# Moving one flag's sum and branch, two query splits, halves of exactness looks, loads and two blocks' attention in a fused attention and feed-forward kernel

## The chip, the cores and the metric

One core of a Trainium2 chip. Its engines run side by side and meet only through semaphores: TensorE (PE; PEld is its weight load), VectorE (DVE), ScalarE (ACT), GpSimd (POOL) and SyncE (SP, which issues the DMAs). The time is device microseconds of one launch; a smaller one is better. Of the kernel before there are three runs, 651.85 to 653.5 us, median 653.43.

## The reference

One post-norm layer on x of 4096 x 256. The attention is linear: K'V is summed over all tokens before any output can be formed. The feed-forward part is gated, with two hidden layers of 1024 x 1024 whose weights are -1, 0 or 1 times a factor.

```python
Q, K, V = x@wq.T, x@wk.T, x@wv.T
context = (Q @ einsum('bnd,bne->bde', K, V)) * sqrt(3/64)
x = layernorm(x + context @ wo.T)
h = silu(tlin(x, w1, s1)) * tlin(x, w2, s2)     # 256 -> 1024
h = gelu(tlin(h, h1, sh1))                      # 1024 -> 1024
h = gelu(tlin(h, h2, sh2))
x = layernorm(x + tlin(h, w3, s3))              # 1024 -> 256
```

## The kernel before

**Tiles.** The 4096 tokens are 8 blocks of 512 (four row tiles of 128), worked on in four pairs p = 0 to 3. Matmuls run in a rounded fp32 format. To keep fp32 accuracy, each operand that is not a weight is a high part (rounded by ScalarE, `hi`, L674, or `hi_of_q`, L618, `hi_of_transposed`, L625) and a low part (the rest, by VectorE, `lo`, L944, `lo_of_q`, L874, `lo_of_transposed`, L885), and each weight tile meets both.

**The hidden layers** (l = 0, 1 of a pair) take seven half-size products in place of eight, as Strassen's scheme does: a weight matrix of 1024 x 1024 is cut in 2 x 2 parts, GpSimd makes sums of those parts once (`combine(i)`, units 0 to 7: four for each hidden weight) and differences of activations in each pair (`differences`, L506 and L516, `further_differences`, L525 and L528). SyncE stores the sums in `combos` in HBM (`store_unit`), copies the plain halves there by `relay_hidden`, and loads one product's weights, 1 MB, into one of three ring slots (`load_ring(g)`). A product is 4 column tiles of 8 matmuls of 512 columns (L1322). Products 0 to 6 of hidden layer L alternate between bank groups B and A; ScalarE copies some out (`copy_out`, L690), VectorE adds others (L951, L957, L963), ScalarE applies gelu (L720).

**Flags.** [...] ScalarE looks: an activation with an accumulated sum of low halves (L569), `bits_of_whole(i)` on a loaded unit (1.06 us), `bits_of_sums(i)` on GpSimd's sums in a long and a short part. For each of seven flags TensorE sums the looks (`flag_sum(s)`, L1211), VectorE turns the sum into a bit (`flag_out(s)`, L866 and L868), and TensorE loads the bit (L1217), compares and branches (L1230): the stage that follows is in the program in an exact and in a plain form. With the reference's data all flags take the exact form. In source order the stages are `front`, `first_l1` and the halves of the first pair's hidden layers.

**The front.** Loads, keys and values, the query projection in 32 pieces, block 0's attention, its residual, layer norm tile by tile (`normalised_tilewise`, VectorE; two of the four last steps are ScalarE's, L631), its transposes (`transposed_first(q)`, L1194) and block 1's attention in two halves. Then `first_l1` runs the gated first layer for blocks 0 and 1: 16 tiles of 4 matmuls (L1262) each, to four banks, with silu (L640) and gate (L938) behind them; a tile's bank must be free, so tile t waits for silu or gate (t - 4)/2. Blocks 2 and 3 get attention and residual (`residual1`, L891) inside pair 0, as later blocks do in the pair before theirs.

**What sets the order.** Every engine's program is written out by hand in one order, with waits on semaphores; nothing is scheduled later. SyncE's queue is in order as well, so a DMA behind a waiting one is late. The change edits these orders.

Of the kernel before, what the change touches and what calls it, by code (L numbers as in the profile page):

```python
# [81 lines left out]
def build(nc, xT_in, xr_in, wkv_src, wq_in, wo_in, w1_in, w2_in, h1_in, h2_in, w3_src, sc_in, s3_in, out):  # L82
# [4 lines left out]
    with ctx:  # L87
# [93 lines left out]
        hidden_relayed = [sem(f"hidden_relayed{l}") for l in range(2)]  # L181
# [92 lines left out]
        def _(sp):  # L274
# [32 lines left out]
            def relay_hidden(l):  # L307

                src = sources[l].rearrange("p (h i n) -> p h i n", h=2, i=KH)[:, :, :, 0:HALF]
                for h in range(2):  # L310
                    sp.dma_start(combos[:, l, 5 + h, :, :], src[:, h, :, :]).then_inc(hidden_relayed[l], 16)
# [12 lines left out]
            def load_ring(g):  # L324
# [3 lines left out]
                if L < 2 and n == 0:  # L328
                    sp.wait_ge(hidden_relayed[L], 32)
# [47 lines left out]
            relay_hidden(1)  # L377
            load_ring(4)
            load_rows_late(2)
            load_ring(5)  # L380
# [178 lines left out]
        def _(act):  # L559
# [162 lines left out]
            def hidden(p, l):  # L722
# [5 lines left out]
                if L == 0:  # L728
                    bits_of_whole(5)
# [83 lines left out]
            for j in range(HC):  # L813
                silu(0, j, A)
                if j == 1:
                    hi_of_q(2)
                if j == 3:
                    hi_of_q(3)
                if j == 0:
                    bits_of_whole(2)  # L820
                if j == 2:
                    bits_of_sums(0)
# [4 lines left out]
                if j == 6:  # L827
                    bits_of_whole(3)
            for j in range(HC):
                silu(1, j, A)  # L830
                if j == 0:
                    bits_of_sums(1)
                if j < KH:
                    hi(0, 1, j)
                if j == 1:
                    bits_of_whole(4)
                if j == 4:
                    bits_of_sums(2)
# [24 lines left out]
        def _(dve):  # L863
# [101 lines left out]
            def hidden(p, l):  # L965
# [91 lines left out]
            def normalised_tilewise(ln, b, add):  # L1057
                y = xr[:, b % 4, :].rearrange("p (t e) -> p t e", e=E)

                for q in range(TPB):  # L1060
# [4 lines left out]
                    nc.vector.bn_aggr(mv[ln][:, ln, q, :], st[ln][:, ln, q, :]).then_inc(tile_aggr[ln], 1)  # L1065
                for q in range(ACT_TILES[ln], TPB):
# [15 lines left out]
            normalised_tilewise(0, 0, attention_residual)  # L1082
            flag_out(1)
# [3 lines left out]
            for j in range(HC):  # L1087
# [3 lines left out]
                if j == 1:  # L1091
                    lo_of_q(2)
                if j == 2:
                    normalise(0, 1, 1)
                if j == 3:
                    lo_of_q(3)
# [36 lines left out]
        def _(pe):  # L1133
# [164 lines left out]
            def product(p, l, n, view):  # L1298
# [3 lines left out]
                for j in range(KH):  # L1302
# [22 lines left out]
                    last.then_inc(prod, 1)  # L1325

# [8 lines left out]
            def with_sums(p, l, view):  # L1335
# [81 lines left out]
            def front(view):  # L1417
# [18 lines left out]
                q_pieces(range(23, 28), view)  # L1436
                pe.wait_ge(q_raw, 2)
# [4 lines left out]
                pe.wait_ge(tile_sum[0], 1)  # L1442
                flag_sum(1)
                transposed_first(2)
                attention_half(0)
                transposed_first(3).then_inc(tr_ready, 1)
                attention_half(1).then_inc(op_ready, 1)
# [12 lines left out]
            def first_l1(view):  # L1460
# [9 lines left out]

                l1(0, A, view, side)
# [60 lines left out]
```

## Time and profile before

| | |
|---|---|
| runs, median (lowest to highest) | 653.43 us (651.85 to 653.5) |
| the profiled execution, its span | 653.65 us, 651.9 us |
| mean granted TensorE clock | 0.998 of full speed |
| TensorE busy | 637.2 us, 98% |
| VectorE, ScalarE, GpSimd busy | 485.7, 410.7, 282.1 us |
| DMA share, 60 to 110 us | 0.92 to 1.03 |

The span runs from the first instruction to the last. A timeline row gives start and duration in us, engine, line, operation, what it writes and reads, the shapes, how many instructions are merged, and in brackets the engine's idle time before it and what ended it. Matmuls overlap: one of 512 columns is shown with 0.39 us and the next starts 0.23 us after it. "issue" is idle time that ended by nothing the profile shows.

### The profile page before, as it was taken

Reading aid. Unit: us, or ns where it says so; the run is one execution under the profiler, and the core shown is the slowest. Engines: PE = TensorE matmul, PEld = TensorE weight load, DVE = VectorE, ACT = ScalarE, POOL = GpSimd, SP = SyncE. Lnnn points to the kernel's source line nnn. Section 1 sums busy time; section 2 is a strip of 40 time slices with the busy share of each in tenths; the row PEclk is TensorE's granted clock in tenths of the full one; section 3 lists DMA queues with packets and bytes.
Section 4 is the critical chain, followed back from the end, with each engine's and each line's share of the span. In section 5 each row is a group of like instructions: output and inputs, shape, how many; then the busy total and the mean of one; then the engine's idle time right before and its main releaser. Section 6 shows DMA issues by size and latency. Waiting matters only on the chain.

```text
span 651.9 us, 9251 instructions
## 1 busy us (share of the span) xinstructions
PE 637.2 (98%) x3191; PEld 534.6 (82%) x3191; DVE 485.7 (75%) x717; ACT 410.7 (63%) x696; POOL 282.1 (43%) x226
## 2 busy tenths in 40 slices
PE   8989999999999999999999999999999999999995
PEld 6867788878889888888889888888889888888885
DVE  4677598789664997798655898698754899488476
ACT  5488789658761666557662657656763457666554
POOL 0367999295000663097000565079000367068034
PEclk9999999999999999999999999999999999999999
DMA  8989999764320036633330035734330015444201
GB/s 327 394 325 341 372 380 348 285 255 164 130 67 1 1 118 220 211 130 130 130 129 1 1 97 167 250 126 168 130 129 2 1 28 188 173 135 160 94 1 66
DMA packets 24370, 103.89 MB, mean 159 GB/s; under 512 B 2224, under 2 KB 3312, under 8 KB 16496
## 3 DMA queue, kind: packets, MB, share of 16 engines
q1 hardware_dynamic: 24032, 102.98, 44.5%
q8 instruction: 29, 0.48, 0.3%
q10 hardware_dynamic: 288, 0.26, 0.1%
q14 instruction: 21, 0.17, 0.1%
HBM read 87.51 MB, written 23.07 MB: 170 GB/s over the span
## 4 chain that ended last, share of the span: by engine, by line
PE 72%; DVE 3%; POOL 1%; issue 1%; ACT 1%; POOLq 0%; DVEq 0%; ACTq 0%
PE ps L1322 49%; PE ps L1262 13%; PE ps L1376 8%; DVE R L944 1%; DVE xr L928 1%; PE ps L1194 1%; PE ps L1182 1%; PE ps L1399 0%; ACT R L674 0%; DVE U L963 0%; POOL rstd L488 0%; POOL quarter L516 0%; ACT quarter L720 0%; POOL rstd L459 0%; POOL quarter L525 0%
## 5 line engine op out<-in xcount | busy, mean ns | idle before, releaser
L1322 PE MATMUL ps<-R,ring 128*128 128x512 f32 x1792 | 410.1, 390 | 1.6 <-DVE fsum L866 1.2
L1322 PEld LDWEIGHTS ps<-R,ring 128*128 128x128 f32 x1792 | 335.2, 188 | 71.6 <-DVE fsum L866 1.6
L944 DVE TENSOR_TENSOR R<-quarter,R 128x512 fp32r<-128x512 f32 x284 | 261.8, 944 | 62.6 <-ACT R L674 62.2
L674 ACT CAST R<-quarter 128x512 fp32r<-128x512 f32 x288 | 175.4, 616 | 30.6 <-POOL quarter L516 12.6
L1262 PE MATMUL ps<-x1T,w 128*128 128x512 f32 x512 | 119.4, 391 | 1.9 <-ACT sg L640 1.1
L720 ACT ACTIVATE quarter<-U,sc 128x512 f32<-128x512 f32 x96 | 69.5, 724 | 74.2 <-DVE U L963 29.4
L1262 PEld LDWEIGHTS ps<-x1T,w 128*128 128x128 f32 x512 | 95.2, 188 | 23.8 <-ACT sg L640 2.7
L506 POOL TENSOR_TENSOR quarter<-quarter,quarter 128x512 f32<-128x512 f32 x32 | 49.6, 1550 | 97.8 <-ACT quarter L720 91.1
L457 POOL TENSOR_TENSOR ve<-mv,eps 128x4 f32<-128x4 f32 x14 | 5.7, 404 | 181.5 <-DVE mv L921 181.5
L640 ACT ACTIVATE sg<-ps,sc 128x512 f32<-128x512 f32 x64 | 44.0, 689 | 61.3 <-PE ps L1262 61.1
L690 ACT COPY U<-ps 128x512 f32<-128x512 f32 x96 | 56.3, 586 | 31.3 <-PE ps L1322 31.3
L938 DVE SCALAR_TENSOR_TENSOR quarter<-ps,sc,sg 128x512 f32<-128x512 f32 x64 | 47.8, 746 | 23.7 <-ACT sg L640 13.4
L516 POOL TENSOR_TENSOR quarter<-quarter,quarter 128x512 f32<-128x512 f32 x32 | 48.9, 1527 | 16.7 <-DVE quarter L938 12.9
L1376 PEld LDWEIGHTS ps<-w,R 128*128 128x128 f32 x448 | 54.7, 192 | 0.7 <-DVE R L944 0.2
L1376 PE MATMUL ps<-w,R 128*128 128x256 f32 x448 | 55.1, 283 | 0.0
L528 POOL TENSOR_TENSOR quarter<-quarter,quarter 128x512 f32<-128x512 f32 x32 | 50.0, 1594 | 0.0
L525 POOL TENSOR_TENSOR quarter<-quarter,quarter 128x512 f32<-128x512 f32 x32 | 48.8, 1554 | 0.0
L928 DVE TENSOR_SCALAR xr<-xr,mv,rstd 128x256 f32<-128x256 f32 x52 | 35.5, 743 | 4.2 <-POOL rstd L459 4.2
L957 DVE TENSOR_TENSOR U<-ps,U 128x512 f32<-128x512 f32 x32 | 22.0, 690 | 14.7 <-PE ps L1322 14.7
L720 ACT ACTIVATE quarter<-ps,sc 128x512 f32<-128x512 f32 x32 | 22.1, 691 | 12.6 <-PE ps L1322 12.6
L963 DVE TENSOR_TENSOR U<-ps,U 128x512 f32<-128x512 f32 x32 | 21.8, 685 | 8.2 <-PE ps L1322 8.2
L446 POOL TENSOR_TENSOR beside<-unit 128x512 f32<-128x512 f32 x8 | 12.2, 1530 | 29.8 <-ACT junk L569 27.7
(84 smaller groups left out, 383.4 us busy)
## 6 DMA issues: line engine op xcount, KB each, us to landing
ring<-combos SPq DMA_DIRECT2D x56, 1024.0 KB, 4.9
combos<-unit SPq DMA_DIRECT2D x8, 1024.0 KB, 7.1
unit<-in_h1T SPq DMA_DIRECT2D x4, 1024.0 KB, 13.9
xr<-in_x_rows SPq DMA_DIRECT2D x8, 512.0 KB, 6.2
unit<-in_h2T SPq DMA_DIRECT2D x4, 1024.0 KB, 12.7
xT<-in_xT SPq DMA_DIRECT2D x7, 512.0 KB, 8.6
out<-xr SPq DMA_DIRECT2D x7, 512.0 KB, 2.9
w<-w_dram SPq DMA_DIRECT2D x3, 1024.0 KB, 7.5
```

What stands on the lines that cost most here:

```text
L506: nc.gpsimd.tensor_tensor(x12[:, c, :], x12[:, c, :], x11[:, c, :], ALU.subtract).then_inc(t_done, 1)
L516: nc.gpsimd.tensor_tensor(t2[:, c, :], x22[:, c, :], x12[:, c, :], ALU.subtract).then_inc(t_done, 1)
L525: nc.gpsimd.tensor_tensor(x11[:, c, :], t2[:, c, :], x11[:, c, :], ALU.subtract).then_inc(t_done, 1)
L528: nc.gpsimd.tensor_tensor(x21[:, c, :], x21[:, c, :], t2[:, c, :], ALU.subtract).then_inc(t_done, 1)
L674: nc.scalar.copy(R[slot_of(p, u)][:, 0, c, :], quarter[operand_home(p, u)][:, c, :]).then_inc(hi_done, 1)
L690: nc.scalar.copy(U[:, 1 if i == 2 else 0, j, :], ps[:, B + j, :]).then_inc(cp_done, 1)
L720: nc.scalar.activation(quarter[dst][:, j, :], src, ACT.Gelu, scale=sc[:, 2 + l, chunk:chunk + 1]).then_inc(gelu_done, 1)
L938: nc.vector.scalar_tensor_tensor(quarter[dst][:, j % KH, :], ps[:, base + (2 * j + 1) % 4, :], sc[:, 1, j:j + 1], sg[:, j % 2, :], ALU.mul ...
L944: nc.vector.tensor_tensor(r[:, 1, c, :], quarter[operand_home(p, u)][:, c, :], r[:, 0, c, :].bitcast(f32), ALU.subtract).then_inc(lo_done, 1)
L1262: last = nc.tensor.matmul(ps[:, base + t % 4, :], w, view(x1T[beta % 2][:, part, c, :]), start=n == 0, stop=n == 2 * EC - 1)
L1322: last = nc.tensor.matmul(ps[:, bank + j, :], w, view(R[slot_of(p, u)][:, part, k, :]), start=n in (0, 1, 5) and k == 0 and part == 0, sto ...
L1376: last = nc.tensor.matmul(rows_of(b)[:, q, :], view(slot[:, part, k, q * P:(q + 1) * P]), w, start=first and k == 0 and part == 0 and q % ...
```

## The change

It moves work; apart from a finer semaphore (one per half of a relay) nothing is added or taken away.

- TensorE: `flag_sum(1)` before the first transpose of block 0; the last two transposes of block 0 and block 1's attention from the end of `front` to the start of `first_l1`, so behind flag 1's load and branch. In every pair but the last, attention of the next pair's blocks goes from behind product 5 to behind its third and its fourth tile.
- VectorE: `flag_out(1)` between the tile statistics and the last two normalisations; `lo_of_q(2)` and `(3)` from the first layer to the first adds of hidden layer 0; the first of its two residuals one step later.
- ScalarE: `hi_of_q(2)` and `(3)` to the same place; the two parts of each look at sums apart; looks at units 3 and 4 one step earlier and later.
- SyncE: relay halves apart, unit 3's store earlier, loads of units 5 and 7 and of the ring changed about.

```diff
-            relay_hidden(0)
+            relay_hidden(0, 0)
             load_unit(4)
             store_unit(2)
             load_ring(0)
+            relay_hidden(0, 1)
+            store_unit(3)
             load_ring(1)
+            load_ring(2)
             load_unit(5)
-            store_unit(3)
             load_unit(6)
-            load_ring(2)
+            load_ring(3)
             load_unit(7)
             store_unit(4)
-            load_ring(3)
-            relay_hidden(1)
             load_ring(4)
+            relay_hidden(1, 0)
             load_rows_late(2)
+            relay_hidden(1, 1)
...
@@ scalar, hidden(p, l)
                 if L == 0:
+                    hi_of_q(2)
+                    hi_of_q(3)
                     bits_of_whole(5)
...
@@ scalar, first layer
             for j in range(HC):
                 silu(1, j, A)
-                if j == 0:
-                    bits_of_sums(1)
+                if j <= 1:
+                    bits_of_sums(1, range(j, j + 1))
                 if j < KH:
                     hi(0, 1, j)
-                if j == 1:
+                if j == 2:
                     bits_of_whole(4)
-                if j == 4:
-                    bits_of_sums(2)
+                if 3 <= j <= 4:
+                    bits_of_sums(2, range(j - 3, j - 2))
...
@@ vector
+                    if L == 0 and j < 2:
+                        lo_of_q(a + j)
...
-                    if L == 0 and j == 1:
+                    if L == 0 and j == 2:
                         residual1(a, B)
...
-            normalised_tilewise(0, 0, attention_residual)
-            flag_out(1)
+            normalised_tilewise(0, 0, attention_residual, lambda: flag_out(1))
...
@@ tensor, with_sums
-                product(p, l, 5, view)
-                if l == 0 and more:
-                    for i in range(2):
-                        pe.wait_ge(gelu_done, n_gelu(L, 1, 2 * i + 1))
-                        attention_out(a + i, lambda q, at=B + 2 * i: ps[:, at + q // 2, q % 2 * E:(q % 2 + 1) * E])
+
+                def attention(j):
+                    if j >= 2:
+                        pe.wait_ge(gelu_done, n_gelu(L, 1, 2 * j - 3))
+                        attention_out(a + j - 2, lambda q, at=B + 2 * (j - 2): ps[:, at + q // 2, q % 2 * E:(q % 2 + 1) * E])
+
+                product(p, l, 5, view, attention if l == 0 and more else None)
...
```

TensorE at the end of the front, before. L1145 are pieces of the query projection, L1211 is flag 1's sum, L1194 a tile's transpose, L1182 half of block 1's attention, and the last three rows are the flag's load and branch:

```order
L1194 MATMUL ps<-ident,xr 128x128 x2
L1145 MATMUL ps<-xhi_112,wqr 128x512 x2
L1194 MATMUL ps<-ident,xr 128x128 x2
L1145 MATMUL ps<-xlo_120,wqr 128x512 x2
L1211 MATMUL ps<-lowf,ones 1x4
L1194 MATMUL ps<-ident,xr 128x128 x2
L1182 MATMUL ps<-T1s,qs_66 128x256 x4
L1194 MATMUL ps<-ident,xr 128x128 x2
L1182 MATMUL ps<-T1s,qs_66 128x256 x4
L1217 TENSOR_LOAD flag
L1217 ISA x2
L1230 COMPARE_AND_BRANCH
```

The same place after; the lines have moved by two:

```order
L1209 MATMUL ps<-lowf,ones 1x4
L1192 MATMUL ps<-ident,xr 128x128 x2
L1143 MATMUL ps<-xhi_112,wqr 128x512 x2
L1192 MATMUL ps<-ident,xr 128x128 x2
L1143 MATMUL ps<-xlo_120,wqr 128x512 x2
L1215 TENSOR_LOAD flag
L1215 ISA x2
L1228 COMPARE_AND_BRANCH
L1192 MATMUL ps<-ident,xr 128x128 x2
L1180 MATMUL ps<-T1s,qs_66 128x256 x4
L1192 MATMUL ps<-ident,xr 128x128 x2
L1180 MATMUL ps<-T1s,qs_66 128x256 x4
```

The sum has moved up by four rows, and load and branch stand ahead of the third transpose.

ScalarE in block 1's first layer, before, from its first silu (L640) on. L569 are looks: unit_125 is unit 4 as loaded, unit_122 and beside_130 are the long and the short part of unit 1's sums; L674 is a high part:

```order
L640 ACTIVATE sg<-ps,sc 128x512
L569 ACTIVATE junk,lowf<-unit_122 128x2048
L569 ACTIVATE junk,lowf<-beside_130 128x512
L674 CAST R_60<-quarter_53 128x512
L640 ACTIVATE sg<-ps,sc 128x512
L674 CAST R_60<-quarter_53 128x512
L569 ACTIVATE junk,lowf<-unit_125 128x1024
L640 ACTIVATE sg<-ps,sc 128x512
L674 CAST R_60<-quarter_53 128x512
L640 ACTIVATE sg<-ps,sc 128x512
L674 CAST R_60<-quarter_53 128x512
L640 ACTIVATE sg<-ps,sc 128x512
```

The same place after:

```order
L570 ACTIVATE junk,lowf<-unit_122 128x2048
L675 CAST R_60<-quarter_53 128x512
L641 ACTIVATE sg<-ps,sc 128x512
L570 ACTIVATE junk,lowf<-beside_130 128x512
L675 CAST R_60<-quarter_53 128x512
L641 ACTIVATE sg<-ps,sc 128x512
L675 CAST R_60<-quarter_53 128x512
L570 ACTIVATE junk,lowf<-unit_125 128x1024
L641 ACTIVATE sg<-ps,sc 128x512
L675 CAST R_60<-quarter_53 128x512
L570 ACTIVATE junk,lowf<-unit_123 128x2048
L641 ACTIVATE sg<-ps,sc 128x512
```

The look at unit 4 has changed sides with the third silu, and the long look at unit 2's sums (unit_123), which followed the fifth silu, now stands ahead of it.

## Rows read from the trace of the kernel before

**Rows 1.** The page, part 1: busy us, share of the span, instructions.

```profile
PE 637.2 (98%) x3191; PEld 534.6 (82%) x3191; DVE 485.7 (75%) x717; ACT 410.7 (63%) x696; POOL 282.1 (43%) x226
```

**Rows 2.** Waits of TensorE, whole span: us in total, times, longest.

```profile
PE ps L1194 <- ACT xr L631: 1.4, 1, 1.4
...
PE ps L1322 <- DVE fsum L866: 1.2, 1, 1.2
```

**Rows 3.** Timeline, 35 to 42 us: start, duration, instruction, idle before.

```profile
37.50 0.18 DVE L1065 BATCH_NORM_AGGREGATE mv<-st 128x2 f32<-128x6 f32 x1
...
38.79 0.44 PE L1194 MATMUL ps<-ident,xr 128*128 128x128 f32 x2
...
39.55 0.38 PE L1194 MATMUL ps<-ident,xr 128*128 128x128 f32 x2
...
39.96 1.07 ACT L625 CAST x1T<-ps 128x512 fp32r<-128x512 f32 x2 [0.67 <-PE ps L1194]
...
40.58 1.29 DVE L885 TENSOR_TENSOR x1T<-ps,x1T 128x512 fp32r<-128x512 f32 x2 [1.13 <-ACT x1T L625]
...
41.08 1.34 PE L1262 MATMUL ps<-x1T,w 128*128 128x512 f32 x4 [0.68 <-ACT x1T L625]
```

**Rows 4.** Line 1217, flag loads: ns min/median/max, starts; all, then 39:41.

```profile
L1217 PEldq TENSOR_LOAD <-flag x7: 298/493/1169, 8.7 to 181.9; - x7
...
L1217 PEldq TENSOR_LOAD <-flag x1: 906/906/906, 39.5 to 39.5; - x1
```

**Rows 5.** Timeline of ScalarE, 57 to 76 us.

```profile
57.88 0.69 ACT L640 ACTIVATE sg<-ps,sc 128x512 f32<-128x512 f32 x1 [0.29 <-PE ps L1262]
58.47 1.90 ACT L569 ACTIVATE junk<-unit 128x2048 uint8<-128x2048 uint16 x1
...
60.49 0.63 ACT L569 ACTIVATE junk<-beside 128x512 uint8<-128x512 uint16 x1
...
61.12 0.60 ACT L674 CAST R<-quarter 128x512 fp32r<-128x512 f32 x1
61.63 0.68 ACT L640 ACTIVATE sg<-ps,sc 128x512 f32<-128x512 f32 x1
...
63.77 1.06 ACT L569 ACTIVATE junk<-unit 128x1024 uint8<-128x1024 uint16 x1 [0.95 <-DMA unit<-in_h2T]
```

**Rows 6.** Timeline of TensorE, from 51 us on.

```profile
51.24 13.23 PE L1262 MATMUL ps<-x1T,w 128*128 128x512 f32 x56
65.55 4.85 PE L1262 MATMUL ps<-x1T,w 128*128 128x512 f32 x20 [1.08 <-ACT sg L640]
...
73.86 5.72 PE L1322 MATMUL ps<-R,ring 128*128 128x512 f32 x24 [0.39 <-issue]
...
79.63 38.38 PE L1322 MATMUL ps<-R,ring 128*128 128x512 f32 x168
```

**Rows 7.** Timeline of VectorE, 70 to 74 us: flag 2.

```profile
71.61 0.14 DVE L866 TENSOR_REDUCE fsum<-ps 1x1 f32<-1x4 f32 x1
71.79 0.14 DVE L868 TENSOR_SCALAR flag<-fsum 1x1 int32<-1x1 f32 x1
```

**Rows 8.** Line 944, low parts: ns min/median/max; then VectorE's timeline, 62 to 96 us.

```profile
L944 DVE TENSOR_TENSOR R<-quarter,R x284: 660/692/1831, 54.4 to 640.3; 128x512 fp32r<-128x512 f32 x142
...
91.71 4.91 DVE L944 TENSOR_TENSOR R<-quarter,R 128x512 fp32r<-128x512 f32 x3 [0.20 <-ACT R L674]
```

**Rows 9.** Line 333, ring loads' landing: issued 40 to 120 us, then at 97.8.

```profile
DMA to landing us min/median/max: 5.3/9.4/13.3
...
DMA to landing us min/median/max: 8.6/8.6/8.6
```

**Rows 10.** Timeline of VectorE, 112 to 142 us.

```profile
119.00 1.23 DVE L891 TENSOR_TENSOR xr<-ps,xr 128x1024 f32<-128x1024 f32 x1 [2.78 <-PE ps L1182]
...
125.55 0.15 DVE L866 TENSOR_REDUCE fsum<-ps 1x1 f32<-1x4 f32 x1 [0.59 <-PE ps L1211]
...
137.71 3.92 DVE L944 TENSOR_TENSOR R<-quarter,R 128x512 fp32r<-128x512 f32 x4
```

More of the change, by code:

```diff
@@ L180, in build @@
         unit_out = [sem(f"unit_out{i}") for i in range(NU)]
-        hidden_relayed = [sem(f"hidden_relayed{l}") for l in range(2)]
+        hidden_relayed = [[sem(f"hidden_relayed{l}_{h}") for h in range(2)] for l in range(2)]
         ring_in = [sem(f"ring_in{k}") for k in range(SLOTS)]
@@ L305, in load_w12, with relay_hidden @@
                 sp.dma_start(w12[:, at:at + EC * HID].bitcast(f32), w12_dram[:, at:at + EC * HID]).then_inc(w12_in[i], 16)
-            def relay_hidden(l):
+            def relay_hidden(l, h):
                 src = sources[l].rearrange("p (h i n) -> p h i n", h=2, i=KH)[:, :, :, 0:HALF]
-                for h in range(2):
-                    sp.dma_start(combos[:, l, 5 + h, :, :], src[:, h, :, :]).then_inc(hidden_relayed[l], 16)
+                sp.dma_start(combos[:, l, 5 + h, :, :], src[:, h, :, :]).then_inc(hidden_relayed[l][h], 16)
             def load_unit(i):
@@ L327, in load_ring @@
                     sp.wait_ge(prod, n_prod((g - SLOTS) // NPROD, (g - SLOTS) % NPROD, KH - 1))
-                if L < 2 and n == 0:
-                    sp.wait_ge(hidden_relayed[L], 32)
+                if L < 2 and n < 2:
+                    sp.wait_ge(hidden_relayed[L][n], 16)
                 if L < 2 and n == 2:
@@ L814, in _ @@
                 silu(0, j, A)
-                if j == 1:
-                    hi_of_q(2)
-                if j == 3:
-                    hi_of_q(3)
                 if j == 0:
                     bits_of_whole(2)
-                if j == 2:
-                    bits_of_sums(0)
+                if 2 <= j <= 3:
+                    bits_of_sums(0, range(j - 2, j - 1))
                 if j == TR1_AFTER:
@@ L826, in _ @@
                     hi(0, 0, j - KH)
-                if j == 6:
+                if j == 5:
                     bits_of_whole(3)
@@ L1055, in _, with normalised_tilewise @@
                                            ALU.mult, ALU.subtract).then_inc(t1_lo, 1)
-            def normalised_tilewise(ln, b, add):
+            def normalised_tilewise(ln, b, add, between=None):
                 y = xr[:, b % 4, :].rearrange("p (t e) -> p t e", e=E)
@@ L1065, in normalised_tilewise @@
                     nc.vector.bn_aggr(mv[ln][:, ln, q, :], st[ln][:, ln, q, :]).then_inc(tile_aggr[ln], 1)
+                if between is not None:
+                    between()
                 for q in range(ACT_TILES[ln], TPB):
@@ L1090, in _ @@
                     stats(0, 1, 1)
-                if j == 1:
-                    lo_of_q(2)
                 if j == 2:
                     normalise(0, 1, 1)
-                if j == 3:
-                    lo_of_q(3)
                 if j > KH:
@@ L1296, in bank_free, with product @@
                     pe.wait_ge(add_done, n_add(L, 1, j))
-            def product(p, l, n, view):
+            def product(p, l, n, view, side=None):
                 L, u = 2 * p + l, NPROD * l + n
@@ L1325, in product @@
                     last.then_inc(prod, 1)
+                    if side is not None:
+                        side(j)
             def hidden(p, l, view):
@@ L1436, in front @@
                 q_pieces(range(23, 28), view)
+                pe.wait_ge(tile_sum[0], 1)
+                flag_sum(1)
                 pe.wait_ge(q_raw, 2)
@@ L1441, in front @@
                 q_pieces(range(30, 32), view)
[L1442 to L1447, printed above, removed]
             def transposed_first(q):
@@ L1469, in flag_side @@
                         flag_sum(2)
+                transposed_first(2)
+                attention_half(0)
+                transposed_first(3).then_inc(tr_ready, 1)
+                attention_half(1).then_inc(op_ready, 1)
                 l1(0, A, view, side)
```

1 line of the change is left out of this document (removed).

## The prediction

> **What bounds the kernel now.** I read the page first. TensorE is busy 98% of the span [rows 1], so a change of order can only win back TensorE's idle time or make more of it. Then I read TensorE's waits: they are few, and all but the last few tenths of a microsecond lie in the first 142 us [rows 2, 3, 6]. Those inside the stretch that the change touches are
>
> - 1.4 us for the first normalised tile of block 0 [rows 2],
> - 0.68 us before the first layer of block 0 [rows 3],
> - 1.08 us inside the first layer of block 1, for a silu [rows 6],
> - 0.39 us ("issue") before the first hidden product [rows 6],
> - 1.2 us in the second product of the second hidden layer, for flag 5's sum on VectorE [rows 2].
>
> That is 4.7 us of 651.9, or 0.7%; no order can give more. The rest of the kernel runs at the matmul's own pitch: 168 matmuls in 38.38 us, 0.228 us each, 7.3 us a product [rows 6]. So each edit is judged by what it does to one of these five waits. The timelines show who is late at each.
>
> **Flag 1, front.** Before, TensorE's program for the front ends with the two last transposes and block 1's attention, and then reads flag 1 and branches. After, it reads the flag and branches first; the transposes come behind the branch. The third tile's transpose ran at 38.79, the fourth's at 39.55, ScalarE's copy at 39.96, the first layer at 41.08 [rows 3]. The order now has the flag between VectorE's last aggregate (ends 37.68 [rows 3]) and the last two normalisations. Reduce and compare take 0.32 us from 71.61 to 71.93 [rows 7], so the bit is there at about 38.0, when TensorE's sequencer has just issued its last projection pieces. The sum itself moves into the 1.4 us wait and costs nothing there; it saved 0.12 us only on a path that no longer decides.
>
> The flag's load costs: seven loads took 0.30 to 1.17 us, and the one in this place 0.91 us, from 39.5 to 40.4 [rows 4]. From the load's end at 40.40 to the first matmul at 41.08 [rows 3] are 0.68 us of compare, branch and first weights. So the third transpose can start at 38.0 + 0.91 + 0.68 = 39.6 instead of 38.79: 0.8 us late. All that follows on the same chain (fourth transpose, ScalarE's two copies, VectorE's low parts, first layer) is late by the same. The gap of 0.68 us before the first layer does not pay for this: the branch was waited for there, but VectorE's low half, needed for the layer's fourth matmul, was itself only ready at 41.87 [rows 3], so that without the branch 0.16 us at most was to be had. With the shortest and the longest load the lateness is 0.2 and 1.06 us. I take 0.8, the row of this very load.
>
> The Trainium skill (DMA: Bandwidth & Descriptors, Latency and other measured facts) gives a tensor load a floor of about 600 ns. By that the lateness is 38.0 + 0.6 + 0.68 - 38.79 = 0.5 us, an estimate from that page. The trace disagrees with a floor: its fastest load took 298 ns [rows 4].
>
> **ScalarE in block 1's first layer.** Before, the look at unit 4 stood ahead of the third silu and waited 0.95 us for the unit's DMA [rows 5]; TensorE then waited 1.08 us for that silu, and the row of 56 matmuls ahead of it had lost 0.3 us against its pitch [rows 6]. After, that look stands behind the third silu, and the two-part looks at the sums are cut in halves. I walk the new queue with the distances between starts in rows 5: silu to next 0.59, long half 2.02, short half 0.63, cast to next 0.51, look at a unit 1.06. silu 0 at 57.88, long half 58.47, cast 60.49, silu 1 61.00, short half 61.59, cast 62.22, silu 2 62.73, cast 63.32, look at unit 4 63.83 (its data were there at 63.75 even in the old DMA order, so no wait), silu 3 64.89, cast 65.48, long half 65.99, silu 4 68.01, which ends at 68.70. When does TensorE want them? Its matmul after the old wait started at 65.55; 1.08 idle, the 0.16 by which a modelled end lies behind the pitch, and the 0.3 lost before it go off: 64.0 for the third silu. That now ends at 63.4, so the wait goes. But the fifth is wanted 16 matmuls later, at 67.7, and there TensorE waits until 68.75: 1.05 us come back, because the long half now stands ahead of the fifth silu and not behind it. 16 matmuls and flag 2's sum (0.12) more, and the layer ends at 72.6 by the pitch, before at 73.3 (the first product's 73.86 less the 0.39 of idle time and the 0.16): 0.7 us gained. Ends: 1.4 us, if that second wait does not show, and 0, if it is as long as both old ones. I take 0.7, the walk.
>
> **Flag 2.** Its gate now follows the sixth silu at 69.23, and ends at 70.7; the bit is there at 71.0, before at 71.93 [rows 7]. Even the longest load, 1.17 us [rows 4], and the 0.68 us from load to matmul give 72.9, and the matmuls end at 72.6. With a load of 0.9 us the branch is hidden: the "issue" wait of 0.39 us [rows 6] goes, 0.45 by my rounding of the pitch. Ends: 0.15 and 0.55.
>
> **Edits that I cost at nothing.** The two query splits leave ScalarE and VectorE in the first layer, where TensorE is not waiting for them except as counted, and go into the second product. Each takes VectorE 0.69 us, or up to 1.83 us by the slowest split of the same kind beside GpSimd [rows 8]; both are 1.4 to 3.7 us. The cover: the last low part of the fourth product's operand ended at about 93.3, as the first of three [rows 8]; its product starts at 73.86 + 3 x 7.3 = 95.8 and wants that part six matmuls, 1.4 us, later. That is 3.9 us. Without cover the cost is the overshoot, some tenths. DMAs: ring loads 1 and 2 now follow the store of unit 3 and the second relay half, but are wanted at 81 and 88 us; the load of unit 7 is queued behind ring load 3, which waits for the first product, about 81; the first to look at that unit is ScalarE in the fourth product, after 97. Unit 5's load goes out behind unit 3's store, some 11 us later than before, and is looked at after 83. Block attention inside product 5 is the same 16 matmuls, so product 6 starts at the same time. It takes away VectorE's 2.78 us wait before the first residual [rows 10]. What is late next: VectorE then waits for flag 4's sum, as it already did for 0.59 us at 125.55 [rows 10], and that matmul stands where it stood. So its third sums, and GpSimd's differences and the low parts up to 141.63 [rows 10], keep their distance to TensorE, and the 1.2 us for flag 5 stays.
>
> **Sum.** +0.8 (front), -0.7 (layer), -0.45 (flag 2): -0.35 us. With the front at 0.2 and the layer at 1.4 it is -1.7, with the front at 1.06 and the layer at 0 about +1.0. The profiled run took 653.65 us around its span of 651.9, so it would be 653.3; it lies 0.2 above the median of 653.43. On the median I forecast 653.1 us.
>
> **Rivals.**
>
> *The gain in the first layer does not come* (the halves only move the wait, and flag 2's load takes its longest): the 0.8 to 1.06 us in front remains, 654.5 us. For it: ScalarE is busy without a gap from 57.88 to the fifth silu in my walk, so a slip of a few tenths lands on TensorE. Against: the 0.95 us DMA wait certainly leaves its place.
>
> *The flag 5 wait goes too*, because VectorE is through with its residuals 2 us sooner: -1.2 us more, 651.9, and with the layer's good end 651.2 us; as this case's time I take 651.3. For it: the 2.78 us wait [rows 10]. Against: VectorE already idled at 125.55 for something the change leaves alone.
>
> *Ring load 5 comes late: slower.* The second half of the second relay, 1 MB, now stands directly ahead of it. Before, it landed 8.6 us after its issue at 97.8 [rows 9], at 106.4, and product 5 starts at 73.86 + 5 x 7.3 = 110.4. The mechanism decides from 4.0 us on. Two more 1 MB pieces' time would do: the nine ring loads of 61 to 118 us landed up to 13.3 us after issue [rows 9], and 98.3 + 13.3 = 111.6 or, with the relay half ahead, up to 114. TensorE would wait 1.2 to 3.6 us: 655.9 us. Against it: before, that load queued behind ring load 4, which is now issued into an emptier queue.
>
> **Chances.** Forecast 0.57; gain missing 0.21; flag 5 too 0.13; ring load 0.09. 0.3% of this kernel is 2.0 us, about what a measurement can tell from none. Faster by more comes from the flag 5 case and a little spread of the runs (651.85 to 653.5): 0.15. Slower comes from the ring case and the upper tail of the second: 0.10. Within 0.3%: 0.75. The likeliest case alone holds 652.3 to 654.5; the range for 8 in 10 is 650.9 to 655.2.
>
> **What would show it.** Right: the third transpose of block 0 behind the flag load at 39.2 to 39.9; first layer at 41.3 to 42.2; TensorE waiting once in block 1's layer, at the fifth silu, for about 1 us; first product 0.1 to 1 us earlier than 73.86; flag 5 still waited for by about 1.2 us. Wrong: a transpose at 38.8 in spite of the branch; no wait at the fifth silu; a DMA as the end of a wait before products 2, 3 or 5; or flag 5's wait gone.

## The result, and the profile after

The changed kernel takes 655.21 us (median of 9 runs, 654.58 to 655.84) against 653.43 us: ratio 1.0034, 95% interval 1.0024 to 1.0044. It is 0.34% slower, just above the 655.2 us at which my range ended; I had forecast 653.1 us and "no change". The profiled run took 655.66 us, span 653.9, 2.0 us more than before. TensorE's row of the page, part 1, to be read against [rows 1]: the same 3191 matmuls are busy 1.2 us longer, and the idle time of the span has grown by 0.8 us.

```profile
PE 638.4 (98%) x3191; PEld 535.3 (82%) x3191; DVE 484.2 (74%) x717; ACT 409.6 (63%) x696; POOL 281.3 (43%) x226
```

TensorE's waits after, as [rows 2]: total, times, longest. Of the lines shown two are new: flag 4's sum waiting for a residual (L890) and a transpose of the front (L1071). One has grown: the wait of a pair's second transposes (L927), 1.0 us in three places, was 0.2 us in one place before.

```profile
PE ps L1320 <- DVE fsum L865: 1.5, 1, 1.5
...
PE ps L1192 <- DVE xr L927: 1.0, 3, 0.5
...
PE ps L1260 <- ACT sg L641: 0.6, 1, 0.6
...
PE ps L1209 <- DVE xr L890: 0.5, 1, 0.5
PE ps L1192 <- DVE xr L1071: 0.5, 1, 0.5
```

TensorE's timeline after, from the front to hidden layer 1, answering [rows 3, 6]:

```profile
39.37 0.43 PE L1192 MATMUL ps<-ident,xr 128*128 128x128 f32 x2 [0.49 <-DVE xr L1071]
...
69.01 1.21 PE L1260 MATMUL ps<-x1T,w 128*128 128x512 f32 x4 [0.62 <-ACT sg L641]
...
73.12 5.60 PE L1320 MATMUL ps<-R,ring 128*128 128x512 f32 x24
...
115.18 1.12 PE L1180 MATMUL ps<-T1s,qs 128*128 128x256 f32 x8
116.13 2.00 PE L1320 MATMUL ps<-R,ring 128*128 128x512 f32 x8
117.97 1.11 PE L1180 MATMUL ps<-T1s,qs 128*128 128x256 f32 x8
118.93 5.63 PE L1320 MATMUL ps<-R,ring 128*128 128x512 f32 x24
125.07 0.19 PE L1209 MATMUL ps<-lowf,ones 128*1 128x4 f32 x2 [0.51 <-DVE xr L890]
...
142.34 16.64 PE L1320 MATMUL ps<-R,ring 128*128 128x512 f32 x72 [1.54 <-DVE fsum L865]
```

The kernel before has product 6 and the tile behind flag 5 here:

```profile
119.76 5.63 PE L1322 MATMUL ps<-R,ring 128*128 128x512 f32 x24
...
141.76 16.62 PE L1322 MATMUL ps<-R,ring 128*128 128x512 f32 x72 [1.16 <-DVE fsum L866]
```

The first product starts 0.74 us earlier than the 73.86 of before, product 6 still 0.83 us earlier (118.93 for 119.76), but the tile behind flag 5 starts 0.58 us later (142.34 for 141.76). So the first pair gave back 1.3 us. VectorE in that stretch, answering [rows 10]:

```profile
120.17 1.21 DVE L890 TENSOR_TENSOR xr<-ps,xr 128x1024 f32<-128x1024 f32 x1
...
121.90 0.68 DVE L956 TENSOR_TENSOR U<-ps,U 128x512 f32<-128x512 f32 x1
123.79 1.23 DVE L890 TENSOR_TENSOR xr<-ps,xr 128x1024 f32<-128x1024 f32 x1 [1.21 <-DMA xr<-in_x_rows]
...
138.29 3.92 DVE L943 TENSOR_TENSOR R<-quarter,R 128x512 fp32r<-128x512 f32 x4
```

The 2.78 us that it idled before its first residual are gone, and it waits 1.21 us for a DMA: block 3's rows.

The other half is in pairs 1 and 2. First the kernel before in pair 1's products 5 and 6 (TensorE's attention in one piece, VectorE's fourth sum L957, TensorE's transposes in one row), then the kernel after (L956):

```profile
271.16 0.69 DVE L957 TENSOR_TENSOR U<-ps,U 128x512 f32<-128x512 f32 x1 [0.53 <-PE ps L1322]
...
270.89 2.08 PE L1182 MATMUL ps<-T1s,qs 128*128 128x256 f32 x16
...
309.10 1.91 PE L1194 MATMUL ps<-ident,xr 128*128 128x128 f32 x16
```

```profile
272.73 0.69 DVE L956 TENSOR_TENSOR U<-ps,U 128x512 f32<-128x512 f32 x1 [1.50 <-PE ps L1320]
...
269.67 1.11 PE L1180 MATMUL ps<-T1s,qs 128*128 128x256 f32 x8
270.62 2.00 PE L1320 MATMUL ps<-R,ring 128*128 128x512 f32 x8
272.46 1.12 PE L1180 MATMUL ps<-T1s,qs 128*128 128x256 f32 x8
...
309.71 1.03 PE L1192 MATMUL ps<-ident,xr 128*128 128x128 f32 x8
311.19 1.06 PE L1192 MATMUL ps<-ident,xr 128*128 128x128 f32 x8 [0.45 <-DVE xr L927]
```

Block a's eight attention matmuls now stand ahead of product 5's fourth tile, so VectorE waits 1.50 us for that tile where it waited 0.53. Its low parts, residuals and third sums, GpSimd's differences and the normalisation of the pair's second block hang on that sum in order, and 38 us later the second transposes wait 0.45 us. (That this chain, and nothing else, carries the loss there is what e1 and e2 test.) From one pair's first layer to the next were 149.95 us before; after it is 150.62 both times. Twice 0.67 is 1.34 of the 2.0 us.

### The profile page after: what moved, and what is told of

Same layout as the page of the kernel before. It is cut to its first block and busy times, and to the rows that moved or that the text cites. A ratio compares the mean times of both kernels' runs of the same rounds, so it can differ in the third digit from the quotient of the medians.

```text
span 653.9 us, 9255 instructions
## 1 busy us (share of the span) xinstructions
PE 638.4 (98%) x3191; PEld 535.3 (82%) x3191; DVE 484.2 (74%) x717; ACT 409.6 (63%) x696; POOL 281.3 (43%) x226
## 5 line engine op out<-in xcount | busy, mean ns | idle before, releaser
L529 POOL TENSOR_TENSOR quarter<-quarter,quarter 128x512 f32<-128x512 f32 x32 | 50.0, 1592 | 0.0
L927 DVE TENSOR_SCALAR xr<-xr,mv,rstd 128x256 f32<-128x256 f32 x52 | 35.5, 744 | 4.2 <-POOL rstd L460 4.2
L956 DVE TENSOR_TENSOR U<-ps,U 128x512 f32<-128x512 f32 x32 | 22.0, 689 | 16.5 <-PE ps L1320 16.5
```

The source lines that it names most:

```text
L529: nc.gpsimd.tensor_tensor(x21[:, c, :], x21[:, c, :], t2[:, c, :], ALU.subtract).then_inc(t_done, 1)
```

## The experiments

Medians of 6 to 12 runs each. Of the kernel before there were 29 to 32 runs per group: 653.10 (e1 to e4), 652.97 (e5 to e8), 653.00 (e9 to e12), 652.74 us (e13 to e15). Ratios are to the kernel before of the same group, and their intervals reach some 0.6 us to either side (e3's 0.9), so that times tell two experiments apart from about 0.9 us on. Smaller differences are read from one trace each. "Lead" is the time from the last query pieces to the first product, 39.09 us before and 38.21 after. It scatters as well: e2 and e10 have the program of the kernel before up to product 5, and leads of 39.33 and 38.75.

**e1: attention inside product 5 in the first pair only.**

```diff
-                product(p, l, 5, view, attention if l == 0 and more else None)
+                product(p, l, 5, view, attention if L == 0 else None)
+                if l == 0 and more and p > 0:
+                    ...   # attention of both blocks, as before
```

> The kernel after, but only the first pair has its attention inside product 5; in pairs 1 and 2 it stands behind product 5 again. Theory (the two later pairs lose 0.67 us each, because the fourth tile of product 5 comes 0.95 us later and VectorE's fourth sums, low parts and the normalisation of the pair's second block follow it): both losses go, pair 1's span is 149.95 again instead of 150.62, the row of the second transposes has no wait of 0.45 us, and the time is 655.2 - 1.35 = 653.9 us. Rival (the later pairs are slower for another reason, for instance the shifted phase against the DMAs): 655.2 us, spans of 150.6 us.

653.76 us, 1.0008 (0.9999 to 1.0018): 1.4 us came back, as the theory had it. VectorE waits 0.52 us for the fourth tile again, and the transposes are one row of 16:

```profile
272.73 0.69 DVE L956 TENSOR_TENSOR U<-ps,U 128x512 f32<-128x512 f32 x1 [0.52 <-PE ps L1320]
...
310.68 1.91 PE L1192 MATMUL ps<-ident,xr 128*128 128x128 f32 x16
```

**e2: the same part alone, on the kernel before.**

```diff
-                product(p, l, 5, view)
-                if l == 0 and more:
+                product(p, l, 5, view, attention if l == 0 and more and p > 0 else None)
+                if l == 0 and more and p == 0:
...
```

> The kernel before, with attention inside product 5 in pairs 1 and 2 alone; the first pair and the front are as before. Theory: it alone costs 0.67 us in each of two pairs, 653.4 + 1.35 = 654.8 us, and the first 180 us of the trace are the same as before. Rival (TensorE has the same matmuls and product 6 starts at the same time, as my prediction had it): 653.4 us.

654.22 us, 1.0013 (1.0004 to 1.0021): 1.1 us slower, with the second transposes at 310.79 behind a wait of 0.45 us. With e1 this half is shown from both sides. Block b's attention stands behind the fourth tile in either order, so by the order the loss is block a's alone; no run moved block a's by itself.

**e3: the second relay half behind block 3's rows.**

```diff
             load_rows_late(2)
-            relay_hidden(1, 1)
             ...
             load_rows_late(3)
+            relay_hidden(1, 1)
             store_unit(7)
```

> The kernel after, but the second half of the second relay (1 MB) is issued behind the load of block 3's rows, not 16 us ahead of it. Theory (block 3's rows land at 123.7 instead of 121.4 because more bytes are queued ahead of them, and VectorE's second residual, flag 4's sum and flag 5's sum are late by it): the rows land near 121, the 0.5 us wait before flag 4's sum goes, flag 5's wait falls from 1.5 us towards 1.2, and 0.5 to 1.3 us come back: 654.2 us. Rival (the second residual is late because block 3's attention or the fourth tile is late): the rows come earlier, the wait stays, 655.2 us.

655.41 us (6 runs), 1.0040 (1.0026 to 1.0054): nothing gained. (The relay stood 13 us ahead of the rows in the kernel after, not 16.) The rows landed at 121.35 and flag 4's wait went, so the DMA part of the theory held. But flag 5's wait grew:

```profile
124.68 0.19 PE L1209 MATMUL ps<-lowf,ones 128*1 128x4 f32 x2
...
141.80 16.62 PE L1320 MATMUL ps<-R,ring 128*128 128x512 f32 x72 [1.84 <-DVE fsum L865]
...
183.34 14.75 PE L1260 MATMUL ps<-x1T,w 128*128 128x512 f32 x64 [0.61 <-issue]
```

The late rows were 0.54 us of the loss at this place (142.34 to 141.80), and most of it was gone again at the last row, whose 0.61 us of idle time the traces of before and after don't have (the last section says what that is). A second chain stood beside the DMA.

**e4: SyncE's order of before**, on the kernel after.

```diff
-            store_unit(3)
             load_ring(1)
-            load_ring(2)
             load_unit(5)
+            store_unit(3)
             load_unit(6)
-            load_ring(3)
+            load_ring(2)
             ...   # and so on to load_ring(7)
```

> The kernel after with SyncE's order of before (relay halves together, unit 3's store behind unit 5's load, ring 3 behind unit 4's store). Theory: block 3's rows land at 121.4 as before, the wait before flag 4's sum goes, the gain of 0.7 us up to the first product stays because ScalarE's own order made it: 654.1 us. Rival 1 (the gain in block 1's first layer came from the DMA order): the first product starts at 73.9 again, 654.9 us or more. Rival 2 (the DMA order changes nothing): 655.2 us.

655.27 us, 1.0031 (1.0021 to 1.0041). Rows at 120.94, flag 5's wait 1.80, as e3. The lead is 38.28 us, as in the kernel after: the gain in the first layers is not SyncE's. The rows in time gave nothing in the runs here either.

**e5: e3, and attention behind product 5 in every pair.**

```diff
-                product(p, l, 5, view, attention if l == 0 and more else None)
+                product(p, l, 5, view)
+                if l == 0 and more:
+                    ...   # attention of both blocks
...
-                    if L == 0 and j == 2:
+                    if L == 0 and j == 1:
                         residual1(a, B)
```

> The kernel of e3 (the second half of the second relay behind block 3's rows), and attention behind product 5 in every pair, the first residual one step earlier, both as before. Theory (a block's attention inside product 5 makes the fourth tile and all that VectorE and ScalarE hang on it late, in the first pair too): the two later pairs gain 1.35 us, and in the first pair the fourth gelu comes 0.8 us earlier and flag 5's wait falls from 1.8 to about 1.1: 655.4 - 1.35 - 0.7 = 653.3 us. Rival (flag 5's wait grew because the two query splits, 2.0 us on VectorE, went ahead of the product 4 and 5 work, and attention is innocent in the first pair): flag 5's wait stays 1.8 us, 654.0 us.

652.52 us, 0.9994 (0.9985 to 1.0002): 2.9 us less than e3, 0.8 more than expected; half a microsecond of it is e3's 0.61. Flag 5's wait is 1.29, so the theory holds in the first pair too. (VectorE waited 0.71 us for block 3's rows, which may be why it isn't 1.16.)

**e6: e3, and the query splits back in the first layer**; attention stays inside product 5.

```diff
                 silu(0, j, A)
+                if j == 1:
+                    hi_of_q(2)
+                if j == 3:
+                    hi_of_q(3)
```

(and `lo_of_q` on VectorE at the same steps, all four gone from `hidden`).

> The kernel of e3, and the query splits of blocks 2 and 3 in the first layer again, on ScalarE and VectorE, as before; attention stays inside product 5. Theory (the splits made VectorE's whole chain of the first pair 2.1 us later, which used up its 2.78 us of idle time before the first residual, so that nothing of it was left to meet the later fourth tile): VectorE's last low part before product 5's sums starts near 106 instead of 108 to 110, it waits again before the residual, and flag 5's wait falls from 1.8 towards 1.1 us; 0 to 0.5 us are lost in the first layer: 655.0 us. Rival (only the fourth tile of product 5 counts): VectorE's chain moves, flag 5's wait stays 1.8 us, 655.4 to 655.9 us.

653.88 us, 1.0016 (1.0007 to 1.0025), 1.5 us less than e3 and 1.1 less than my theory, with flag 5's wait at 1.18 (half a microsecond of the rest is e3's 0.61, as in e5):

```profile
140.30 16.64 PE L1324 MATMUL ps<-R,ring 128*128 128x512 f32 x72 [1.18 <-DVE fsum L867]
```

So in the first pair either undoing takes the growth of the wait away (to 1.29 and 1.18): the two parts clash.

**e7: the new front alone, on the kernel before.**

```diff
-            normalised_tilewise(0, 0, attention_residual)
-            flag_out(1)
+            normalised_tilewise(0, 0, attention_residual, lambda: flag_out(1))
...
+                transposed_first(2)
+                attention_half(0)
+                transposed_first(3).then_inc(tr_ready, 1)
+                attention_half(1).then_inc(op_ready, 1)
                 l1(0, A, view, side)
```

(with `flag_sum(1)` ahead of `transposed_first(0)`.)

> The kernel before with the change of the front alone: flag 1's sum, bit, load and branch ahead of the third transpose of block 0. Theory (my step of 0.8 us, 0.6 us in the trace after): the third transpose at 39.4 and not 38.8, the block's layer 0.56 us later, and all of it is still there at the end: 653.1 + 0.56 = 653.7 us. Rival (ScalarE sets the pace of block 1's layer, so that what the front loses is taken from the wait of 1.08 us there): 653.1 us, and that wait is about 0.5 us.

652.59 us, 0.9995 (0.9986 to 1.0004): the rival. The third transpose is late as expected (39.60), but the wait of 1.08 us in block 1's layer is gone entirely:

```profile
39.60 0.43 PE L1195 MATMUL ps<-ident,xr 128*128 128x128 f32 x2 [0.65 <-DVE xr L1070]
...
52.02 18.10 PE L1263 MATMUL ps<-x1T,w 128*128 128x512 f32 x76
```

That wait is ScalarE's look at unit 4, a DMA that lands at 63 to 64 us whatever TensorE does (63.75 before, 63.10 here): what is lost in front of it is not waited there. Part of this is luck. In the four other traces with the front and the two orders of before (e2, e9, e10, e13), that load landed at 63.29 to 64.02 and the wait was 0.77 to 1.37 us. The lead is 38.36, no worse than with ScalarE's new order: with the new front, that order gained nothing that this trace shows.

**e8: flag 5's bit behind the first low part**, on the kernel after.

```diff
-                    if L == 1 and j == KH - 1:
+                    if L == 1 and j == 0:
                         flag_out(5)
```

> The kernel after, but VectorE turns flag 5's sum into a bit behind the first of four low parts and not behind the fourth. Theory (what the first pair loses all gathers in TensorE's wait for flag 5's sum, which is late only because VectorE's queue is): the sum, made at 135.0, is reduced near 139.3, the wait of 1.54 us at 142.3 goes, and if product 2 finds its low parts in time the kernel takes 655.2 - 1.5 = 653.7 us. Rival (the low parts behind it, the ones product 2 needs, end no earlier, so the wait moves to product 2's first matmul): the wait stands at about 142.6 with VectorE's low part as its end, and the time is 654.9 us or more.

655.35 us, 1.0034 (1.0023 to 1.0045): no change. The wait for flag 5 is gone, and 9 us later TensorE waits for ScalarE's copy instead; the second transposes wait longer (0.62):

```profile
151.27 7.56 PE L1320 MATMUL ps<-R,ring 128*128 128x512 f32 x32 [1.05 <-ACT U L691]
```

Flag 5 shows the lateness of VectorE, GpSimd and ScalarE; it doesn't make it. The rival was right in kind, though the wait moved further than it said.

**e9 and e10: on the kernel before, the late splits alone, and attention inside product 5 in the first pair alone.** The edit of e9 on ScalarE (the same two splits are gone from the first layer, and VectorE's move likewise), then e10's, which also has the first residual one step later:

```diff
                 if L == 0:
+                    hi_of_q(2)
+                    hi_of_q(3)
                     bits_of_whole(5)
...
-                product(p, l, 5, view)
-                if l == 0 and more:
+                product(p, l, 5, view, attention if L == 0 else None)
+                if l == 0 and more and p > 0:
...
```

> The kernel before with one part of the change alone: the query splits of blocks 2 and 3 go from the first layer to the second product, on ScalarE and VectorE. Theory (the splits and attention inside product 5 draw on the same 2.78 us that VectorE idled before its first residual; either alone finds them free): VectorE's low parts of the first pair are 2.0 us later, its wait before the residual shrinks to about 0.7 us, flag 5's wait stays 1.2 us, the time stays 653.0 us. Rival (the splits alone cost what e6 gave back, 1.4 us, by making ScalarE and VectorE late before product 4): 654.4 us.

> The kernel before with attention inside product 5 in the first pair alone, the first residual one step later. Theory (as for e9: the 2.78 us are free, VectorE's two residuals come out in time): flag 5's wait stays 1.2 us, the fourth gelu starts about when it did (122.7), 653.0 us. Rival (the fourth tile of product 5, 0.95 us later, is what counts in this pair as in the later ones): flag 5's wait grows by 0.6 us or more, 653.7 us.

652.40 us, 0.9993 (0.9983 to 1.0003), and 652.54 us, 0.9993 (0.9984 to 1.0002). Each costs nothing, flag 5's wait is 1.16 and 1.17, and each eats VectorE's 2.78 us: with the splits 0.45 are left (first fence, e9); with attention early, VectorE is so far ahead that it waits for block 3's rows (second, e10), and the fourth gelu starts at 120.29, not at the 122.7 that I expected.

```profile
118.69 1.23 DVE L889 TENSOR_TENSOR xr<-ps,xr 128x1024 f32<-128x1024 f32 x1 [0.45 <-PE ps L1178]
```

```profile
121.21 1.23 DVE L891 TENSOR_TENSOR xr<-ps,xr 128x1024 f32<-128x1024 f32 x1 [0.96 <-DMA xr<-in_x_rows]
```

**e13: both edits together, on the kernel before.**

> The kernel before with the splits late (e9) and attention inside product 5 in the first pair (e10) together. Theory A (they clash only because TensorE was 0.8 us ahead in the kernel after: VectorE's queue, walked with the distances of e9 and e10, has its fourth sum at 121.9 and ScalarE the fourth gelu at 122.6, just when the kernel before has it): flag 5's wait stays near 1.2 us, 652.5 to 653.0 us. Theory B (together they cost 0.7 us wherever TensorE stands): flag 5's wait is 1.8 us or more, 653.2 to 653.7 us.

653.42 us, 1.0005 (0.9997 to 1.0014). The median stands in B's range, and by the ratios the two together cost 0.8 us over either alone; the wait for flag 5, 1.45 us, stands between A and B. The traces of nine kernels with their rows in time or nearly so put it in one line; "gelu behind product 6" is the start of ScalarE's fourth gelu of product 5 less the start of product 6:

| | first product less last query pieces | gelu behind product 6 | wait for flag 5 |
|---|---|---|---|
| e10 | 38.75 | 0.82 | 1.17 |
| e6, e15 | 38.25, 37.79 | 2.73, 2.74 | 1.18, 1.16 |
| before, e9, e12 | 39.09, 38.68, 37.79 | 2.90 | 1.16 |
| e13 | 38.60 | 3.26 | 1.45 |
| e4 | 38.28 | 3.61 | 1.80 |
| e3 | 38.40 | 3.64 | 1.84 |

The traces of e2, e7 and e14 too are at 2.90 us with waits of 1.16 to 1.17; e5, at 2.90 with 1.29, and the four with rows later still (after, e1, e8, e11) are not in the table.

Up to 2.9 us the wait is 1.16; from about 2.97 on it grows by what the gelu is later (1.45, 1.80 and 1.84 less 1.16, taken off 3.26, 3.61 and 3.64, give 2.96 to 2.97). Behind that gelu ScalarE has 3.9 us of look and gelu work (122.66 to 126.54 before) ahead of its first gelu of the third sums, which VectorE delivers then.

With splits and attention both in, VectorE's sums no longer wait for TensorE but seem to follow from GpSimd's differences: the fourth gelu starts 32.94 to 32.97 us behind the start of their last run (L528 before, L529 after) in all seven traces with both parts, and that run starts as late as ever (89.21 before, 89.65 after). No run moved GpSimd's work alone, so this link is read, not shown. Counted from the last query pieces, the gelu then hardly moves (87.89 us before, 87.70 after, 87.77 in e13), while product 6 comes earlier (84.99, 84.02, 84.51): A's mechanism, with a threshold that e13 had passed already, since its TensorE was 0.5 us ahead of the kernel before's.

```profile
122.66 0.72 ACT L720 ACTIVATE quarter<-U,sc 128x512 f32<-128x512 f32 x1
...
122.61 0.72 ACT L721 ACTIVATE quarter<-U,sc 128x512 f32<-128x512 f32 x1 [1.10 <-DVE U L956]
```

(Fourth gelu, before, then after.)

**e11: the kernel after with the old front.**

```diff
+            normalised_tilewise(0, 0, attention_residual)
+            flag_out(1)
...
+                flag_sum(1)
+                transposed_first(2)
                 ...   # the rest at the end of front, as before
```

> The kernel after with flag 1's sum, bit, load and branch behind the transposes again, as before. Theory (the new front makes the third transpose 0.6 us late; in the order of before that was hidden in the look's wait for unit 4, which lands at 63 to 64 us whatever the front does, but in the kernel after unit 4 is there by 59.4 and ScalarE's queue follows TensorE, so nothing hides it): everything from the first layer on is 0.56 us earlier, 655.2 - 0.56 = 654.7 us. Rival (the front is free in the kernel after too, as it was in e7): 655.2 us.

655.11 us, 1.0029 (1.0018 to 1.0039): the runs can't tell 0.56 us from nothing. The trace has the theory's gain. The lead is 37.78, 0.43 us better, GpSimd's last differences and the fourth gelu come earlier by as much (0.43 and 0.46 us from the last query pieces on), and up to the next pair's first layer there are 147.97 us, 148.54 in the kernel after. So the front isn't free in the kernel after, as far as one trace shows.

**e12: the edits of e3, e5, e6 and e11 together.** Of the change there remain ScalarE's looks, SyncE's order and the finer semaphore.

> A version to beat both: the kernel after with the old front, the query splits back in the first layer, attention behind product 5 in every pair with the first residual one step earlier, and the second half of the second relay behind block 3's rows. What is left of the change is ScalarE's order in the first layer and most of SyncE's. Theory (e5's 652.5 us, less 0.56 for the front and 0.1 for flag 5's wait): 651.9 us, first product at 72.6 if keys begin as in the trace before, flag 5's wait 1.2 us, pair 1's span 149.95. Rival (the splits were moved to make room for the new order in the first layer, and put back they cost it 0.5 us or more): 652.5 us or more, with a longer wait at a silu.

652.49 us, 0.9991 (0.9982 to 1.0000): 0.6 us more than the theory's time, though its rows came, and the rival's longer wait at a silu did not (0.63 us, in the kernel after 0.62). Wait for flag 5 1.16, pair spans as before, first product 72.58. The profiled span is 650.7, 1.2 us under that of before; the runs show half of it.

**e14: e12 with the new front.**

> The kernel of e12 with the new front (flag 1's sum, bit, load and branch ahead of the third transpose). Theory (with unit 4 loaded early nothing in block 1's layer hides the front's 0.6 us, and with attention and splits where they were nothing in the first pair does): first product 0.56 us later against the last query pieces, and 652.5 + 0.56 = 653.05 us. Rival (the front is free, as e7 and e11 seemed to say): 652.5 us.

652.64 us, 0.9997 (0.9988 to 1.0005). The last query pieces start at 34.78, in e12 at 34.79; the first product, e12 then e14:

```profile
72.58 5.60 PE L1325 MATMUL ps<-R,ring 128*128 128x512 f32 x24
```

```profile
73.06 5.60 PE L1324 MATMUL ps<-R,ring 128*128 128x512 f32 x24
```

0.48 us in the trace, 0.5 in the span; the ratios' intervals overlap, so the runs alone don't show it. All eight traces with the new front and ScalarE's new order have leads of 38.21 to 38.84 (38.84 is e1, where flag 1's load took 1.39 us; the others end at 38.40), the three with the old front 37.78 to 37.79. The five with the front and ScalarE's order of before have 38.60 to 39.33. So with the old front ScalarE's order gains 0.8 us or more.

**e15: e12 with attention inside product 5 in the first pair** (`attention if L == 0 else None`).

> The kernel of e12 with attention inside product 5 in the first pair, the first residual one step later. Theory (with the splits early VectorE has room, as in e6, whose wait for flag 5 was 1.18 us): the same time as e12, 652.5 us, flag 5's wait 1.2 us. Rival (the fourth tile's 0.95 us count here too): flag 5's wait 1.6 us or more, 653.1 us.

652.26 us, 0.9990 (0.9982 to 0.9999), flag 5's wait 1.16. Free when the splits are early. It has the lowest median of all versions, 0.1% under the kernel before and about 0.4% under the kernel after; its interval overlaps those of e5, e7, e9, e10, e12 and e14, so it isn't shown to be faster than they are.

## Why the prediction was wrong, by its own steps

- *Flag 1, front: +0.8.* Right mechanism and place: the bit was ready at 38.04, the load took 0.80 us, and 0.49 more to the transpose, not 0.68. It was 0.58 us late. The first layer's first matmul came at 41.26, only 0.18 late and before my 41.3 to 42.2, but at block 1's transposes the lateness is 0.56 again (51.01 for 50.45), and e14 gives 0.48 at the first product. Mis-sized by 0.2 to 0.3.
- *ScalarE in block 1's layer: -0.7.* Right: the wait for the third silu went and one at the fifth came, 0.62 us for my 1.05.
- *Flag 2: -0.45.* Right; its load took 0.30 us and the branch was hidden. Up to the first product my sum was -0.35; the trace has -0.74 (about +0.56, -0.75 and -0.55 in these three terms), and -0.88 from the last query pieces.
- *"Block attention inside product 5 is the same 16 matmuls, so product 6 starts at the same time."* **The step that failed.** Product 6 did start on time, but the fourth tile of product 5 did not, and VectorE and ScalarE work tile by tile. I looked at who waits for attention and not at who waits for the tile behind it. In pairs 1 and 2, which I never walked, it is +1.34 us in the trace (e1 gave 1.4 back, e2 lost 1.1). [Rows 10] had a 2.78 us wait in the first pair; pair 1's fourth sum waited 0.53 us for TensorE's tile itself, which was there to be read.
- *The query splits, cost nothing.* True alone (e9). But I gave both them and the attention the same idle time: 2.0 us of splits, and attention that takes the wait away, against one wait of 2.78. With TensorE 0.8 us ahead they cost about 0.7 (e5, e6, the table).
- *"Third sums, differences, low parts keep their distance to TensorE."* Failed: they stood still in time or came later (the low parts ahead of flag 5's bit at 138.29 for 137.71). So the gain of the first layers could not pass the first pair, and flag 5's wait took it.
- *DMAs.* Ring load 5, my slower rival, landed at 109.27, in time. Block 3's rows, which the same list of DMAs delays from 121.42 to 123.69, I didn't look at: flag 4's wait of 0.51 us, and 0.54 at flag 5 by e3's trace. In the runs neither e3 nor e4 gained by rows in time.

From the last query pieces to the end, then: -0.9 up to the first product, +1.35 back in the first pair (up to the next pair's first layer 148.54 us for 148.07), +1.34 in the later pairs, and 0.14 of start, together the 2.0 us of the two spans. Of the first pair's part the late rows hold little at that place: e3 and e4 have 148.43 and 148.24 there. Splits with attention hold the rest: e5 and e6, which undo one of the two, have 147.26 and 147.11. The rival "flag 5's wait goes too" had the sign wrong (the wait grew from 1.16 to 1.54 us); e8 shows that even without it nothing is won.

## What to carry to other kernels

When work is slipped between the tiles of a product, ask who consumes the next tile, in every iteration of the loop and not only in the one with a visible idle stretch. An idle stretch on a helper engine can be spent once: add up all parts of a change that draw on it. And a gain early in a kernel lasts only while every engine's queue can follow; one that is anchored to something else (here, it seems, GpSimd's differences, and a DMA) turns it into a wait further on, where it looks like the fault of whatever flag stands there.

## What the runs showed of the hardware

A flag's load on TensorE's queue depended on the DMA order. In all seven traces with SyncE's order of before, flag 2's load took 0.79 to 1.17 us and flag 3's 0.78 to 1.25; in all ten with the new order both took 0.30 to 0.32. Here is flag 2's in the kernel after and then in e4, which differ in SyncE's order alone (ns):

```profile
L1215 PEldq TENSOR_LOAD <-flag x1: 303/303/303, 71.4 to 71.4; - x1
```

```profile
L1215 PEldq TENSOR_LOAD <-flag x1: 1037/1037/1037, 71.0 to 71.0; - x1
```

What the load contends with wasn't tried. Flag 1's load, at 38 to 40 us, took 0.44 to 1.39 us, with either order. The Trainium skill (DMA: Bandwidth & Descriptors, Latency and other measured facts) gives a tensor load a floor of about 600 ns; loads of 0.30 us stand in all 17 traces, below it.

Behind the last flag's load the first matmul of the next stage starts 0.59 to 0.67 us after the load's end in all 17 traces. What varies is when the load begins: from 0.50 us ahead of the last hidden matmul (e10) to 0.04 us behind it (e3), though the bit is ready 3.7 to 4.2 us before the load in every trace. So TensorE's step from the last hidden matmul to the next stage's first is 0.40 us in e10, 0.51 and 0.54 in the kernels before and after, and 1.00 in e3, whose "issue" wait is this. Why the load begins when it does wasn't tried, and it follows no part of the change. Half a microsecond is as much as most terms here, so single spans are no better than that.
